# Projecting two heads at once from rows moved by DMA, with the adjacency turned after its count, in a sparse graph-attention kernel

## The reference

```python
h = jnp.maximum(_layernorm(x, axis=-1), 0.0)
q, k, v = h @ Wq + bq, h @ Wk + bk, h @ Wv + bv        # 8 heads of 64
scores = einsum('bmhd,bnhd->bhmn', q, k) / 8 + edge_bias[adj]
scores = leaky_relu(scores, 0.2)
scores = where(adj > 0, scores, -1e9)
attn = softmax(scores, axis=-1)
out = einsum('bhmn,bnhd->bmhd', attn, v)
return x + out @ Wp + bp
```

## Time and profile before

| | |
|---|---|
| median of 3 runs | 1035.78 us (1034.2 to 1037.22) |
| the profiled execution, its time | 1032.86 us |
| its span, first to last instruction | 1030.6 us |
| mean granted TensorE clock | 0.990 of full speed |
| PE, PEld busy | 978.6 us (95%), 965.4 us (94%) |
| DVE, ACT, POOL busy | 914.2 (89%), 776.0 (75%), 487.2 us (47%) |
| DMA | 125.2 MB in 190760 packets |

### The profile page before, as it was taken

The page is one execution under the profiler, slowest core; times in us unless marked ns, Lnnn a source line. Parts: engine busy times, 40 slices in busy tenths (PEclk is TensorE's granted clock), DMA queues, the critical chain, the costliest instruction groups (busy, mean ns, idle before and its releaser), DMA issues.

```text
span 1030.6 us, 28703 instructions
## 1 busy us (share of the span) xinstructions
PE 978.6 (95%) x9056; PEld 965.4 (94%) x9056; DVE 914.2 (89%) x3409; ACT 776.0 (75%) x1737; POOL 487.2 (47%) x865
## 2 busy tenths in 40 slices
PE   4578999999999999999999999999999999999996
PEld 4468999999999999999999999999999999999995
DVE  3878899889998999898998899989998899989984
ACT  3587787788778787887777777878777887788762
POOL 1004455455545454554554455545454545555454
PEclk9989999999999999999999999999999999999998
DMA  7574534344343444434343343435343344433220
GB/s 175 184 227 122 145 107 131 104 114 136 113 133 114 121 127 116 134 104 143 103 130 108 113 145 101 137 103 151 104 137 103 109 132 121 135 113 109 77 70 9
DMA packets 190760, 125.20 MB, mean 121 GB/s; under 512 B 32832, under 2 KB 180300, under 8 KB 190604
## 3 DMA queue, kind: packets, MB, share of 16 engines
q1 hardware_dynamic: 189812, 122.75, 40.9%
q10 hardware_dynamic: 792, 0.53, 0.3%
HBM read 79.19 MB, written 44.04 MB: 120 GB/s over the span
## 4 chain that ended last, share of the span: by engine, by line
PE 84%; DVE 9%; issue 2%; DMA 1%; ACT 1%; POOL 1%; SPq 0%; ACTq 0%; POOLq 0%; DVEq 0%
PE bank L1222 20%; PE bank L1253 11%; PE bank L1175 10%; PE bank L1210 8%; PE bank L1164 6%; PE bank L1312 6%; PE bank L1165 5%; PE bank L1187 5%; PE bank L1199 5%; PE bank L1230 3%; DVE w L1658 2%; PE bank L1238 1%; DVE w L1681 1%; DVE o_all L1757 1%; PE bank L1298 1%
## 5 line engine op out<-in xcount | busy, mean ns | idle before, releaser
L1034 POOL TENSOR_SCALAR a_line<-w,a_bias 128x256 f32<-128x256 f32 x512 | 263.3, 514 | 453.3 <-DVE w L1681 411.3
L1222 PE MATMUL bank<-pt,nat_sb 128*65 128x128 f32 x2048 | 265.4, 273 | 0.2
L1658 DVE CUSTOM_DVE_ANT_0 w<-bank,mask_rows 128x256 f32<-128x256 f32 x512 | 195.9, 418 | 60.9 <-issue 56.8
L1441 ACT ACTIVATE pt<-bank 128x512 f32<-128x512 f32 x256 | 153.9, 601 | 110.9 <-PE bank L1175 105.9
L1681 DVE SCALAR_TENSOR_TENSOR w<-w,shift,a_line 128x256 f32<-128x256 f32 x512 | 229.9, 488 | 2.5 <-POOL a_line L1034 2.5
L1222 PEld LDWEIGHTS bank<-pt,nat_sb 128*65 128x65 f32 x2048 | 230.7, 138 | 0.6 <-issue 0.6
L1670 DVE TENSOR_TENSOR onehot<-val,counts_to 128x512 fp32r<-128x512 f32 x256 | 181.1, 707 | 2.2
L1423 ACT ACTIVATE mask_own<-bank,mask_bias 128x512 bf16<-128x512 f32 x256 | 175.1, 684 | 1.1 <-PE bank L1199 1.1
L1175 PE MATMUL bank<-ident,w 128*128 128x128 f32 x1024 | 154.0, 273 | 0.0
L1432 ACT ACTIVATE t_sb<-bank 128x512 fp32r<-128x512 f32 x256 | 150.2, 587 | 2.7 <-PE bank L1187 2.6
L1164 PE MATMUL bank<-t_sb,q_hi 128*128 128x256 f32 x512 | 142.8, 301 | 1.1 <-DVE wmax L1658 1.0
(11 more groups left out here) (135 smaller groups left out, 1619.5 us busy)
## 6 DMA issues: line engine op xcount, KB each, us to landing
adj_in<-in_adj_dram SPq DMA_DIRECT2D x64, 512.0 KB, 4.0
mask_store<-mask_own SPq DMA_DIRECT2D x64, 512.0 KB, 3.5
mask_rows<-mask_store SPq DMA_DIRECT2D x512, 64.0 KB, 2.4
nl_store<-nl_ring SPq DMA_DIRECT2D x7, 512.0 KB, 4.1
stack_store<-stage SPq DMA_DIRECT2D x7, 512.0 KB, 2.9
h_stack<-stack_store SPq DMA_DIRECT2D x7, 512.0 KB, 4.5
h_nl<-nl_store SPq DMA_DIRECT2D x28, 128.0 KB, 3.6
x_res<-in_x_dram SPq DMA_DIRECT2D x16, 128.0 KB, 2.3
```

The costliest lines, as they stand in the source:

```text
L1034: nc.gpsimd.tensor_scalar(a_line[:, i % 2, :], w[:, i, :], 5.0, a_bias[:, i:i + 1], ALU.mult, ALU.add)\
L1222: last = pe.matmul(o_part[0:D + 1, P * u:P * u + P], nat_sb[:, t % 2, p % 4 * 2 + u, k, :], pt[:, p % 2, u, k, :], start=(k == 0), stop=(k ...
L1658: nc.vector.tensor_tensor_reduce(w[:, i, :], row_bank[:, SLOTS * u:SLOTS * u + SLOTS], mask_rows[:, t % 2, p % 4 * 2 + u, :], 0.25, LEAST_ ...
```

## The change

- **Projection.** Two heads share one matmul. SP moves ScalarE's result (now called `o_turned`) by two DMAs per tile into `o_pairs`, even heads in partitions 0 to 63 and odd heads in 64 to 127, and by a third DMA the row of sums of the 8 heads into 8 partitions of `den_rows`. `project` then issues two matmuls of 128 rows for each part (128 columns stationary, 128 moving) against `w_pair`, a block-diagonal 128x128 matrix for each pair of heads, and in part 0 one more, 8 partitions deep and 8 columns wide, that turns the sums.
- **Steps.** `MOVE_O = 26`; PROJ 27 to 28, NORM 28 to 29, SUM 30 to 31, OUT 31 to 32.
- **Norm.** The sums of all eight heads are clamped and inverted in part 0; part 1 is one scaling. The wait for the previous tile's sum stands ahead of the addition to x.
- **Adjacency.** COUNT stays at 6 and TURN_A goes from 5 to 7; POOL's `convert` also waits for the transposes of two tiles before.
- **Masks.** The store stays at step 14 and the eight spreads have a step of their own, 15.
- `w_sum` has two parts, and `vec` is two accumulating matmuls in place of one. The same replacement of `w_ext` stands in the setup and in the dense programs, which do not run on this data.

```diff
-    LOAD, CONV, TURN_A, COUNT, USED, RANK, VAL, ONEHOT = 0, 4, 5, 6, 7, 8, 9, 9
+    LOAD, CONV, COUNT, TURN_A, USED, RANK, VAL, ONEHOT = 0, 4, 6, 7, 7, 8, 9, 9
-    MASK, MASK_OUT, TFILL, QFILL, BETA, COLSUM, VEC = 10, 14, 13, 9, 6, 18, 22
-    SCORE, A_LINE, Y, TURN, PV, X_ADD, PROJ, NORM, SUM, OUT = 17, 19, 20, 21, 22, 24, 27, 28, 30, 31
+    MASK, MASK_OUT, MASK_IN, TFILL, QFILL, BETA, COLSUM, VEC = 10, 14, 15, 13, 9, 6, 18, 22
+    SCORE, A_LINE, Y, TURN, PV, X_ADD, MOVE_O, PROJ, NORM, SUM, OUT = 17, 19, 20, 21, 22, 24, 26, 28, 29, 31, 32
...
-            def move_masks(b, t):
+            def store_masks(b, t):
...
+            def spread_masks(b, t):
+
+                par, before = t % 2, MT * b + t // 2
+                own = mask_store[par].rearrange("(g r s) -> r g s", r=P + GQ, s=SLOTS)[0:GQ]
                 if later(before):
                     sp.wait_ge(scores_taken, 8 * (TPG * b + t) - 8)
                 sp.wait_ge(mask_stored[par], 16 * before + 16)
                 for h in range(H):
                     sp.dma_start(mask_rows[GQ * h:GQ * h + GQ, par], own).then_inc(mask_in[par], 16)
 
+            def move_o(b, t):
+
+                n, par = TPG * b + t, t % 2
+                sp.wait_ge(o_copied, 4 * n + 4)
+                if later(n, 2):
+                    sp.wait_ge(proj_done, 2 * n - 2)
+                heads = o_turned[0:D, par].rearrange("p (c a) q -> p c a q", a=2)
+                for a, rows in enumerate((slice(0, D), slice(D, P))):
+                    sp.dma_start(o_pairs[rows, par], heads[:, :, a]).then_inc(o_moved[par], 16)
+                sp.dma_start(den_rows[0:H, par], o_turned[D:D + 1, par]).then_inc(o_moved[par], 16)
...
+                t = tile(b, s, MOVE_O)
+                if t is not None:
+                    move_o(b, t)
                 t = tile(b, s, MASK_OUT)
                 if t is not None:
-                    move_masks(b, t)
+                    store_masks(b, t)
+                t = tile(b, s, MASK_IN)
+                if t is not None:
+                    spread_masks(b, t)
...
             def project(b, t, e, s):
                 n = TPG * b + t
-                pe.wait_ge(o_copied, 4 * n + 4)
-                free(adj_bank_uses, b, s, len(list(adj_bank_uses(b, s))) - 1)
-                for h in range(4):
-                    last = pe.matmul(adj_bank[:, (D + 1) * h:(D + 1) * h + D + 1], ot_sb[0:D + 1, t % 2, 4 * e + h, :],
-                                     w_ext[0:D + 1, 4 * e + h, :], start=True, stop=True)
+                pe.wait_ge(o_moved[t % 2], 48 * (n // 2) + 48)
+                free(adj_bank_uses, b, s, 0)
+                for c in range(2):
+                    last = pe.matmul(adj_bank[:, P * c:P * c + P], o_pairs[:, t % 2, 2 * e + c, :], w_pair[:, 2 * e + c, :],
+                                     start=True, stop=True)
+                if e == 0:
+                    last = pe.matmul(adj_bank[:, 2 * P:2 * P + H], den_rows[0:H, t % 2, :], ident[0:H, 0:H],
+                                     start=True, stop=True)
                 last.then_inc(proj_done, 1)
...
                 if i == 0 and later(TPG * b + t, 2):
-                    act.wait_ge(proj_done, 2 * (TPG * b + t) - 2)
+                    act.wait_ge(o_moved[t % 2], 48 * ((TPG * b + t) // 2))
...
                 dve.wait_ge(proj_done, 2 * n + e + 1)
-                if e == 0 and later(n):
-                    dve.wait_ge(summed, n)
-                parts = adj_bank[:, 0:4 * (D + 1)].rearrange("p (h d) -> p h d", d=D + 1)
-                nc.vector.tensor_scalar(den[:, heads], parts[:, :, D], 1e-30, None, ALU.max).then_inc(den_ready, 1)
+                parts = adj_bank[:, 0:2 * P].rearrange("p (h d) -> p h d", d=D)
                 if e == 0:
-                    nc.vector.tensor_scalar(alone[:, :], parts[:, 0, D:D + 1], 0.5, None, ALU.is_lt).then_inc(alone_ready, 1)
-                dve.wait_ge(den_ready, 2 * n + e + 1)
-                nc.vector.reciprocal(den_inv[:, heads], den[:, heads]).then_inc(den_inv_ready, 1)
-                if e == 0:
+                    sums = adj_bank[:, 2 * P:2 * P + H]
+                    nc.vector.tensor_scalar(den[:, :], sums, 1e-30, None, ALU.max).then_inc(den_ready, 1)
+                    nc.vector.tensor_scalar(alone[:, :], sums[:, 0:1], 0.5, None, ALU.is_lt).then_inc(alone_ready, 1)
+                    dve.wait_ge(den_ready, n + 1)
+                    nc.vector.reciprocal(den_inv[:, :], den[:, :]).then_inc(den_inv_ready, 1)
...
+                    if later(n):
+                        dve.wait_ge(summed, n)
...
-                dve.wait_ge(den_inv_ready, 2 * n + e + 1)
-                nc.vector.tensor_tensor(o_all[:, heads, :], parts[:, :, 0:D],
-                                        den_inv[:, heads].unsqueeze(2).to_broadcast([P, 4, D]), ALU.mult)\
+                    dve.wait_ge(den_inv_ready, n + 1)
+                nc.vector.tensor_tensor(o_all[:, heads, :], parts, den_inv[:, heads].unsqueeze(2).to_broadcast([P, 4, D]), ALU.mult)\
                     .then_inc(proj_taken, 1)
...
-                    pe.matmul(misc[:, 0:D], mean_rep[:, :], w_sum[:, :], start=True, stop=True).then_inc(vec_done, 1)
+                    for a in range(2):
+                        last = pe.matmul(misc[:, 0:D], mean_rep[:, :], w_sum[:, a, :], start=(a == 0), stop=(a == 1))
+                    last.then_inc(vec_done, 1)
```

More of the change, by code:

```diff
@@ L80, in preln_graph_attention @@
         w = sb("w", [P, 2 * RING, SLOTS], F32, fast)
-        ot_sb = sb("ot_sb", [P, 2, H, P], F32, fast)
+        o_turned = sb("o_turned", [P, 2, H, P], F32, fast)
         pt = sb("pt", [P, 2, 2, 2, P], F32, fast)
@@ L101, in preln_graph_attention @@
         mean_rep = sb("mean_rep", [P, P], F32, fast)
-        w_sum = sb("w_sum", [P, D], F32, fast)
+        w_sum = sb("w_sum", [P, 2, D], F32, fast)
         g_hi = sb("g_hi", [P, H, 2, D], F32R, fast)
         g_lo = sb("g_lo", [P, H, 2, D], F32R, fast)
-        w_ext = sb("w_ext", [P, H, D + 1], F32, fast)
+        w_pair = sb("w_pair", [P, PAIRS, P], F32, fast)
+        o_pairs = sb("o_pairs", [P, 2, PAIRS, P], F32, fast)
+        den_rows = sb("den_rows", [P, 2, P], F32, fast)
         both_halves = sb("both_halves", [P, D], F32R, fast)
@@ L258, in preln_graph_attention @@
         o_copied = sem("o_copied")
+        o_moved = [sem(f"o_moved{i}") for i in range(2)]
         proj_done = sem("proj_done")
@@ L666, in dense_scalar @@
                 for rows in (slice(0, D), slice(D, P)):
-                    nc.scalar.activation(vp_hi[rows, :].rearrange("p (h d) -> p h d", h=H), w_ext[0:D, :, 0:D],
-                                         ACT.Copy).then_inc(v_weights, 1)
+                    for a, heads in enumerate((slice(0, D), slice(D, P))):
+                        last = nc.scalar.activation(vp_hi[rows, :].rearrange("p (c a d) -> p a c d", a=2, d=D)[:, a],
+                                                    w_pair[heads, :, D * a:D * a + D], ACT.Copy)
+                    last.then_inc(v_weights, 1)
                 def q_hi_parts(b, k):
@@ L738, in dense_vector @@
                 for rows in (slice(0, D), slice(D, P)):
-                    nc.vector.tensor_tensor(vp_lo[rows, :].rearrange("p (h d) -> p h d", h=H), w_ext[0:D, :, 0:D],
-                                            vp_hi[rows, :].rearrange("p (h d) -> p h d", h=H).bitcast(F32), ALU.subtract)\
-                        .then_inc(v_weights, 1)
+                    for a, heads in enumerate((slice(0, D), slice(D, P))):
+                        lo, hi = (part[at, :].rearrange("p (c a d) -> p a c d", a=2, d=D)[:, a]
+                                  for part, at in ((vp_lo, rows), (vp_hi, heads)))
+                        last = nc.vector.tensor_tensor(lo, w_pair[heads, :, D * a:D * a + D], hi.bitcast(F32), ALU.subtract)
+                    last.then_inc(v_weights, 1)
                 def add_beta(g):
@@ L1115, in adj_bank_uses @@
             def adj_bank_uses(b, s):
+                t = tile(b, s, COUNT)
+                if t is not None:
+                    yield cnt_ready, TPG * b + t + 1
                 t = tile(b, s, TURN_A)
@@ L1118, in adj_bank_uses @@
                     yield adj_copied, TPG * b + t + 1
-                t = tile(b, s, COUNT)
-                if t is not None:
-                    yield cnt_ready, TPG * b + t + 1
                 due = piece(b, s, PROJ, 2)
@@ L1275, in step @@
                     natural(b, p)
+                t = tile(b, s, COUNT)
+                if t is not None:
+                    count(b, t, s)
                 t = tile(b, s, TURN_A)
@@ L1278, in step @@
                     turn_adj(b, t, s)
-                t = tile(b, s, COUNT)
-                if t is not None:
-                    count(b, t, s)
                 due = piece(b, s, PROJ, 2)
@@ L1447, in copy_o @@
                 if i == 0 and later(TPG * b + t, 2):
-                    act.wait_ge(proj_done, 2 * (TPG * b + t) - 2)
```

(9 more changed lines are left out.)

14 lines of the change are left out of this document (6 added, 8 removed).

## The result

The changed kernel takes 1050.39 us (median of 4 runs, 1047.82 to 1055.8), the one before 1034.99 us beside it on the same chip (1034.14 to 1037.22). The ratio is 1.0157, with a 95% interval of 1.0122 to 1.0193: slower by 15 us, where 994.5 us and a gain of 40 were forecast. The execution profiled took 1047.82 us.

What follows compares the result with a forecast made beforehand. PE was taken to set the pace, DVE close behind. Projection -44.2, adjacency -3.0, `vec` +1.9, ramp +1.5, tail +2.5 sum to -41.3 from 1032.86: 991.6, plus 2.9 for the median gives 994.5 us; range 984 to 1014.

Steps and rivals of the forecast that it cites:

- the floor of 13.3 us a tile: DVE's least time per tile: 14.85 less 1.14 idle less 0.41 for one clamp and reciprocal fewer.
- the cushion of 0.8: Per tile, DVE's 13.3 us against PE's 14.1, so PE should still decide; called the forecast's narrow place.
- My last paragraph: The prediction's list of signs, including that it is wrong if PE idles for `o_all` or moved rows at `project`.
- cushion of 0.0 to 1.2 us: What remains of 2.8 us before DVE reads the masks, after later store, moves' transfers and faster tile: hidden, barely.
- rival at 0.08: The masks come late: 2.5 us of delay gives 14.5 us a tile and 1019 us; chance 0.08.
- The large records: The new projection's eight full-height matmul records on PE: 0.115 us each, 0.92 us a tile.
- streaming adds: Rival on PE's projection: streaming adds to the load, 0.175 us a record, 1026 us; chance 0.05.
- loads do not overlap: Rival on PE's projection: full-height loads do not overlap, 0.224 us a large record, about 1053 us; chance 0.04.
- The small matmul: The matmul turning the sums in `project`, 8 deep and 8 wide: two records of 0.115 us, 0.23 us a tile.
- The -3 us: Gain from turning the adjacency after its count: half of PE's 6.5 us idle ahead of the transposes.
- Ramp and tail: Start and end of the run: +1.5 us (0 to 4) for the ramp, +2.5 us (0 to 5) for the tail.
- DVE keeps its share of waits: Rival: DVE's 7.7% idle time is needed for handshakes, so 14.4 us a tile and 1013 us; chance 0.14.

Runs made afterwards that it cites:

- the order alone: Kernel before, with its old projection and no new DMAs, in the steps of the changed kernel: 1086.09 us, 1.0492.
- the last version: Changed kernel with norm first, mask store first, sums' matmul 128 deep, POOL's addition three steps later, subtraction one step later: 991.66 us, 0.9589.
- the old phases: Changed kernel with its projection steps three later (PROJ 31, NORM 32, SUM 34, OUT 35) and TURN_A back at 5: 1026.05 us, 0.9922.

## Why the prediction was wrong, step by step

**The step that failed** is the one on DVE: "Part 0 leaves the step that also has query rows, one-hot and shifts, its fullest, for the next; the load is spread better", and from it the floor of 13.3 us a tile and the cushion of 0.8. It counted DVE's work of a whole tile, and not where in a step each piece stands against PE's. The old place of part 0's norm was in DVE's fullest step, but PE's part 1 came late enough for it. In the kernel before (part 0, the end of its norm, part 1):

```profile
507.56 1.08 PE L1253 MATMUL bank<-w_ext,ot_sb 65*128 65x65 f32 x8
...
510.95 0.42 DVE L1757 TENSOR_TENSOR o_all<-bank,den_inv 128x256 f32<-128x256 f32 x1
...
511.65 1.08 PE L1253 MATMUL bank<-w_ext,ot_sb 65*128 65x65 f32 x8
```

Counted from part 0's first record, in the median of 47 tiles, the norm ended after 3.88 us there and PE was ready for part 1 after 4.08. In the changed kernel the norm ends after 4.16 and PE is ready after 3.68: the query pieces, which stood between the two parts, now come behind part 1, and DVE runs late in that step. With the norm first it ends after 3.42 us, ahead of PE's 3.68. The cushion was 0.2 us, it shrank from both sides, and the forecast had no term for it. I had looked at the wait of `count` behind part 1's norm and at `project` part 0's inputs, never at part 1 behind part 0's norm, which I had quoted as 3.0 us of the old kernel. My last paragraph names the sign ("if PE idles for `o_all` ... at `project`"), without a rival for it. Shown: 25 us come back when the norm alone is moved, and the order alone, without the new projection, loses 51, of which the same move returns 48.

**The second half of that step** is the floor's durations. I took DVE's times per instruction as fixed. In the changed kernel they grew: `w` from 488 ns to 532, `shift` from 223 to 365, `shift_neg` from 228 to 280. Its busy time per tile is 371.98 / 400 x 14.97 = 13.9 us, where 369.30 / 400 x 14.85 = 13.7 less 0.41 was expected. Shown: with POOL's addition three steps later, the same instructions take 34 us less. The Trainium skill, "SBUF — State Buffer", section "SBUF: two separate sides", says that a GpSimd instruction that reads SBUF and a VectorE instruction with two SBUF inputs exclude each other at one port pair, the later one waiting. The rows agree: the three that grew have two SBUF inputs or more, the 58 long ones end when POOL's instruction does, others with two SBUF inputs got shorter in the new order (`onehot` from 707 ns to 688, `x_res` from 330 to 254), and `take_scores` (418 and 420 ns) and `o_all` (419 and 419), which read PSUM, kept their times. That it is this port is the Trainium skill's account; the runs show that such instructions grow beside POOL's work and that the place of that work decides. Why the conversion, whose step didn't change, now falls on `shift_neg` was not tried by itself. With the addition moved, such long ones fell from 58 to 24, but in the last version, which has it moved too, there are 68, and it is the fastest: the long shifts alone don't set the time.

**Subtraction.** A dependence that I overlooked: with `TURN_A` at 7, the copy that the subtraction at step 7 needs is made in that step. It costs 9 us alone, and 12.7 once PE and DVE are close again.

**Masks.** Forecast: cushion of 0.0 to 1.2 us, "hidden, barely", rival at 0.08. Measured: eight waits, 11.3 us in all, and 11 us of the time. The issues were mis-sized: 507.07 - 504.93 = 2.1 us ahead of the store instead of 1.4 (the first two took 1.29 us and the third 0.71), so the store went out 1.1 us after the last copy (505.96), where 0.5 was my mark. The spreads took 4.46 us in this tile, 3.95 in the median, where 3.64 was the median before. But an ordinary tile bears that: its masks landed 2.2 us ahead of DVE's read (median of 47 tiles of 14.97 us; 2.8 before). The eight waits are the first tile's and the last one's (3.2 and 3.3 us) and those of the first tile of six graphs (4.7 together), and for these a term was missing. SP waits there for the output store to land:

```profile
293.03 0.47 SPq L900 DMA_DIRECT2D out_dram<-x_res  x1
297.30 0.37 SPq L895 DMA_DIRECT2D x_res<-in_x_dram  x1
...
298.33 1.29 SPq L930 DMA_DIRECT2D o_pairs<-o_turned  x2
...
300.47 0.37 SPq L910 DMA_DIRECT2D mask_store<-mask_own  x1
```

With `OUT` at 32 that wait, 3.4 to 4.6 us (2.1 to 3.9 before), stands right ahead of the moves. In the six tiles the mask store left 2.6 to 3.8 us after the last copy. In the runs with `OUT` at 35 and the moves still first (the old phases, and POOL's addition later) none of the six waits is left. So the rival had the sign, but not this mechanism, and it is one loss of several here.

**The projection on PE.** The large records were right: four in 0.44 us in part 1, 0.11 us each; loads of 128 rows lie beside the streaming. That settles the rivals "streaming adds" and "loads do not overlap" against them, and with the second the rule of the Trainium skill quoted in the prediction ("TensorE: Matmul & The Clock Gate"; it stands there in the section "The mechanism"): by it they would stand 0.22 us apart. The prediction also took from it that the change would lose, but the old records, each loaded into the same 65 rows, would by that rule not have overlapped either, and at 0.115 us a record they did. The small matmul was mis-sized: I put 0.23 us and took 0.11 to 0.23 as its bounds, and part 0 took 0.62 + 0.31 = 0.93 us against 0.44 without it, 0.49. So the projection is 1.37 us a tile, not 1.15, and PE's saving 0.47 x 64 = 30 us, not 44.

**The transposes.** Right: their wait is 0.0. The -3 us were lost elsewhere, since the bank's wait only changed its place.

**Ramp and tail.** The ninth tile's count is 2.9 us later (151.45 against 148.51); 1.5 forecast, within 0 to 4. After the last count, at 974.51, come 71.5 us instead of 1030.6 - 964.96 = 65.6: 5.9 more, against 2.5 and a bound of 5. PE's wait for the last moved rows is 3.1 us of that stretch and DVE's wait for the last tile's masks 3.3; in the kernel before neither was there.

**Sum.** 14 us less from PE than forecast, and four losses that are not in the sum. Lifted one at a time they are worth 25, 26, 11 and 9 us, more together than the gap of 56, because the first two meet in one wait. All lifted, and the small matmul 128 deep (which makes the projection 0.53 + 0.14 + 0.44 = 1.11 us, about the forecast's 1.15), the tile has the forecast's 14.1 us and the run its 994.5 less 3. The forecast was thus about right for a change that fits DVE's, POOL's and SP's order to the new steps, and wrong for this one. The nearest rival was "DVE keeps its share of waits": the engine is right, its 1013 us is not, and the slower side came by a mechanism that I hadn't listed.

## What to carry to other kernels

When a step is moved, list for each instruction in it whom it releases on the other engines, and read from the timeline how late its engine runs at the new place; a floor from busy time per tile says nothing of that. Where two engines share a resource, look at which instructions fall together in the new order, since durations change with it. And when a shorter bottleneck gains nothing, try the order inside a step first: moving three lines returned 25 us here.

## What the runs showed of the hardware that was not expected

- A two-record fp32 matmul 8 partitions deep behind 128-deep ones costs more than one 128 deep: 0.62 + 0.31 us for part 0 against 0.53 + 0.14, with the same output.
- The place of POOL's additions, with no instruction added, changes DVE's busy time by 34 us (927.2 and 893.4), and beside POOL's work a DVE instruction of 4 columns takes 0.66 us in place of 0.16. POOL's own 128x256 addition takes 1071 ns at the one place and 731 at the other.
- Three moves between SBUF tiles hold SP for 2.1 us, 0.65 to 0.71 us each, where the spreads of masks took 0.45; with the mask store issued ahead of them, seven of DVE's eight waits for masks went.
- Taking 17 us of work off PE gave 2.8 us while PE was busy 396.8 of 400 us and DVE 380.2: the busy time alone did not tell that DVE set the pace, since that of PE holds latency. The waits show in the distance between starts, 0.83 us from part 1 to the query pieces where the records need 0.44.
